# Two experts' lists instead of two ranks' lists, with tokens handed on from the lower expert's chunk to the higher one's list

## The chip, the cores and the metric

The kernel runs on one core of one Trainium2 chip. A core has a matrix engine (PE, with its weight loads listed as PEld), a vector engine (DVE), a scalar engine (ACT), GpSimd (POOL) and a sync engine (SP) that here only issues transfers. PE writes to PSUM banks, DMA moves data between DRAM and SBUF. The metric is the device time of one launch in microseconds, lower is better. Each launch computes the whole layer for one seed.

## The reference

```python
xn = _layernorm(x)                                         # x: 3125 x 256
x = x + gnn(xn, src, dst) + linear_attention(xn)           # 53125 edges, 8 heads
tokens = _layernorm(x)
probs = softmax(tokens @ router_w.T)                       # 8 experts
rw, re = top_k(probs, 2); rw = rw / rw.sum(-1)
out = tokens
for e in range(8):
    h = gelu(tokens @ w1[e] + b1[e])                       # 256 x 256, exact gelu
    out = out + combine[:, e:e + 1] * (h @ w2[e] + b2[e])
x = x + out
```

So a token's result is a sum of three parts: x + tokens, and two experts' outputs, each with its weight. The order of the two experts does not matter.

## The kernel before, in words

**Up to 283 us** the first layernorm, the projections, the edge counts and the graph sum are worked out. `rows` [125, 25, 261] keeps all tokens: token `t * 125 + p` is in row p of tile t.

**Routing (283 to 328 us)** goes over six groups of up to five tiles (`ROUT`). For a group DVE adds the graph part (`add_graph`), takes mean and variance (`scale`), picks the two best experts (`choose`: max, max_index, and `oh`, a one-hot of each rank's expert), and works out where in a list each token stands (`weigh`: `slot_i`, one row number for rank 0 and one for rank 1). A row of `rows` holds 256 normalized values, the token's number, its two weights and what undoes the normalization (std + 1, mean). POOL sends tile t with `send(t, r2)` (L545): an indirect transfer that writes each of 125 rows at its own row number in the DRAM table `xs`, one region for each rank. A list of an expert starts and ends on whole chunks of 128 rows, filled up with rows `null` that SP stored during the graph stage (L390); a null row carries a token number that is out of bounds, so that it is written nowhere. After each group's rank 0 sends one rank 1 send follows (`BETWEEN`), after the last group eight (up to `EARLY` = 13), and the other 12 stand in POOL's queue behind the chunks 0, 2, ... 22.

**The table (322 to 328 us)**: on one partition DVE turns the counts of each expert's tokens into an expert and a first row for each of 64 chunks (L1089 to L1121), then `table_done`.

**The expert stage (from 339.7 us)** runs 64 chunks, `MC` = 32 for rank 0 and then 32 for rank 1. 3125 tokens in eight lists never need more than 32 chunks; what the data do not need are null chunks, which take the same steps. For chunk c: SP reads its first row into a register (L393) and loads 128 rows into one of six buffers `xch` (L396), which it may do once `ys_done` says that chunk c - 6 was weighed. The first load waits for all rank 0 sends to have landed (`sent[0]`). PE transposes the rows (`turn_rows`, L1471), runs the first layer (L1482) after the turn of the next chunk but one, and the second (L1491, L1493). ACT copies the transposed rows (L693), applies gelu (L701) and, in the first half, undoes the normalization in the buffer (`restore`, L707). DVE copies the weights of the chunk after next (L1131, L1132) and weighs (`weigh_rows`): L1142 takes the token numbers, L1144 writes restored row + weight x output into `ys` (L1147 weight x output alone in the second half). POOL writes `ys` to `out` (`add_rows`): L560 plainly in the first half, L563 as an adding transfer in the second, once all of the first half's have landed. PE's program fixes the order: at step c it turns chunk c + 2, runs the first layer of c + 1 and the second of c. `keep_clock` (L1167) are matmuls without use, 20 of them behind `table_done`, ahead of the first turn.

## Time and profile before

| what | us |
|---|---|
| median of three runs (492.91 to 498.22) | 496.13 |
| the profiled execution | 495.52 |
| its span in the profile | 493.8 |
| PE busy | 443.1 |
| DVE busy | 320.3 |
| ACT busy | 282.8 |
| POOL busy | 238.0 |

The span runs from the first to the last instruction of the program; the profiled execution's own time is 1.7 us longer. Busy shares are averages over stages with different limits, so the stages have to be looked at one by one. PE is the busiest engine, but its matmuls are pipelined and their ends are modelled, so what PE waits for, and what waits for PE, says more than its busy time.

### The profile page before, as it was taken

How to read it: one execution, taken by the hardware profiler on the slowest of the kernel's cores; microseconds unless marked ns; L12 is line 12 of the kernel's file. 1: busy time of each engine (PE TensorE's matmuls, PEld its weight loads, DVE VectorE, ACT ScalarE, POOL GpSimd, SP SyncE). 2: the span in 40 equal slices, each digit the busy share in tenths (PEclk: the TensorE clock that was granted, in tenths of full speed). 3: DMA queues.
4: the chain of work that ended last, by engine and by line, in shares of the span. 5: the costliest groups of instructions: out<-in, count | busy, mean ns of one | idle time of the engine just before them, and what ended most of it. 6: DMA issues, size and time to landing. Idle time of an engine off the chain costs nothing.

```text
span 493.8 us, 10033 instructions
## 1 busy us (share of the span) xinstructions
PE 443.1 (90%) x3289; PEld 327.2 (66%) x3289; DVE 320.3 (65%) x869; ACT 282.8 (57%) x632; POOL 238.0 (48%) x261
## 2 busy tenths in 40 slices
PE   2899999989999999999989997845998989999993
PEld 1787787755666665556645655614877878999982
DVE  3687779687777777677713897570655656666662
ACT  2757455757777776777734686403655547444441
POOL 5057683481111111111100057887676764688886
PEclk9999999999999999999998989658999999999998
DMA  8844005554777776576670013335444443367763
GB/s 217 178 134 133 13 16 171 174 134 120 150 150 150 150 151 156 144 145 134 134 133 2 1 49 91 87 87 147 122 129 132 125 130 98 81 110 123 118 104 36
DMA packets 119300, 57.52 MB, mean 116 GB/s; under 512 B 92647, under 2 KB 116435, under 8 KB 119248
## 3 DMA queue, kind: packets, MB, share of 16 engines
q1 hardware_dynamic: 104688, 41.63, 35.9%
q0 software_dynamic: 13744, 14.39, 14.4%
q10 hardware_dynamic: 816, 0.85, 0.7%
q8 instruction: 27, 0.44, 0.4%
q14 instruction: 25, 0.20, 0.1%
HBM read 19.14 MB, written 19.14 MB: 78 GB/s over the span
## 4 chain that ended last, share of the span: by engine, by line
PE 73%; DVE 7%; DMA 6%; issue 4%; ACT 4%; POOL 3%; SPq 1%; POOLq 0%; another core or an unknown queue 0%; DVEq 0%; ACTq 0%
PE bank L1482 12%; PE bank L1273 12%; PE bank L1493 11%; PE bank L1224 9%; PE bank L1304 4%; PE bank L1191 4%; PE bank L1200 3%; PE bank L1471 3%; DMA region_a<-region_a 3%; PE bank L1207 2%; PE bank L1167 2%; DMA rows<-in_x 2%; PE bank L1491 2%; PE bank L1284 2%; POOL xs L545 2%
## 5 line engine op out<-in xcount | busy, mean ns | idle before, releaser
L615 ACT CAST region_a<-bank 128x500 bf16<-128x500 f32 (+1 forms) x175 | 112.2, 668 | 46.1 <-PE bank L1224 41.9
L545 POOL DMA_INDIRECT xs<-rows,slot_i x50 | 61.9, 1237 | 49.8 <-issue 44.3
L1273 PE MATMUL bank<-region_a,region_z 125*64 125x500 bf16 (+1 forms) x525 | 71.1, 367 | 2.6 <-DMA region_a<-region_a 2.6
L1482 PE MATMUL bank<-region_a,region_c 128*128 128x128 f32 x512 | 70.1, 280 | 2.9 <-issue 2.0
L516 POOL COPY wide<-den 125x256 f32<-125x256 f32 x25 | 12.9, 516 | 119.4 <-DVE den L923 119.4
L1224 PEld LDWEIGHTS bank<-region_a 128*128 128x128 bf16 x625 | 41.2, 101 | 42.6 <-issue 31.0
L1482 PEld LDWEIGHTS bank<-region_a,region_c 128*128 128x128 f32 x512 | 63.3, 194 | 5.7 <-issue 3.8
L1224 PE MATMUL bank<-region_a 128*128 128x125 bf16 x625 | 64.8, 220 | 1.6 <-ACT region_a L615 1.3
L1493 PE MATMUL bank<-region_c,region_a 128*128 128x256 f32 x256 | 65.7, 379 | 0.0
L701 ACT ACTIVATE region_a<-bank,region_c 128x128 f32<-128x128 f32 x128 | 40.3, 367 | 40.7 <-PE bank L1482 28.4
L563 POOL DMA_INDIRECT out<-region_a x32 | 55.4, 1730 | 12.4 <-issue 8.5
L1131 DVE COPY region_c<-region_w 128x1026 f32 x64 | 46.9, 733 | 17.1 <-issue 16.3
L693 ACT COPY region_a<-bank 128x256 f32<-128x256 f32 x64 | 24.0, 375 | 44.8 <-issue 23.0
L1493 PEld LDWEIGHTS bank<-region_c,region_a 128*128 128x128 f32 x256 | 43.7, 190 | 4.0
L862 DVE TENSOR_TENSOR region_a<-iota,locs 128x3200 bf16<-128x3200 bf16 x25 | 45.9, 1835 | 0.0
L560 POOL DMA_INDIRECT out<-region_a x32 | 33.1, 1035 | 24.8 <-DVE region_a L1144 14.6
L856 DVE TENSOR_TENSOR region_a<-iota,keys 128x3150 bf16<-128x3150 bf16 x25 | 44.7, 1790 | 0.0
L1142 DVE CAST region_a<-region_a 128x1 int32<-128x1 f32 x64 | 9.8, 153 | 50.3 <-issue 33.4
L1273 PEld LDWEIGHTS bank<-region_a,region_z 125*64 125x64 bf16 x525 | 24.8, 110 | 22.3 <-DMA region_a<-region_a 3.2
L1167 PE MATMUL bank<-zeros,ones 128*128 128x512 bf16 x108 | 31.9, 447 | 6.8 <-DVE expert_i L1121 6.8
L1191 PE MATMUL bank<-wzkv,region_a 128*125 128x320 f32 x100 | 32.2, 445 | 0.0
L465 POOL TENSOR_SCALAR rows<-rows,rstd,shift 125x256 f32<-125x256 f32 x25 | 19.2, 776 | 23.6 <-DVE region_a L749 23.5
(219 smaller groups left out, 764.9 us busy)
## 6 DMA issues: line engine op xcount, KB each, us to landing
region_a<-xs SPq DMA_DIRECT2D x64, 130.5 KB
region_w<-in_w SPq DMA_DIRECT2D x4, 1024.0 KB, 9.1
rows<-in_x SPq DMA_DIRECT2D x5, 560.0 KB
xs<-null SPq DMA_DIRECT2D x16, 130.5 KB
xs<-null SPq DMA_DIRECT2D x2, 913.5 KB
out<-region_a POOLq DMA_INDIRECT x64
xs<-rows,slot_i POOLq DMA_INDIRECT x50
wzkv<-in_WkvT ACTq DMA_DIRECT2D x1, 512.0 KB, 6.4
```

What stands on the lines that cost most here:

```text
L545: nc.gpsimd.indirect_dma_start(xs, bass.IndirectOffsetOnAxis(slot_i[:, t, r2:r2 + 1], 0), rows[:, t, :], None).then_inc(sent[r2], 16)
L563: nc.gpsimd.indirect_dma_start(out, to, ys[:, c % 4, :], None, bounds_check=N - 1, oob_is_err=False, compute_op=ALU.add).then_inc(added[c ...
L615: nc.scalar.copy(to, count_bank(n)[:, 0:w * TP].rearrange("p (c t u) -> p c t u", c=w, t=NT)).then_inc(adj_done, 1)
L856: nc.vector.tensor_tensor(koh[:, t % 2, :, :].rearrange("p c (m u) -> p c m u", u=2), counting(KW), columns(keys, t, KW), ALU.is_equal).th ...
L862: nc.vector.tensor_tensor(loh[:, t % 2, :, :].rearrange("p c (m u) -> p c m u", u=2), counting(P), columns(locs, t, P), ALU.is_equal).then ...
L1131: nc.vector.tensor_copy(wc[:, c % 3, :].rearrange("p (a f) -> p a f", a=1), w_all[:, bass.ds(e, 1), :])
L1167: nc.tensor.matmul(ps[:], ones16[:], zeros[:], start=True, stop=True)
L1191: last = nc.tensor.matmul((y0, y1)[s][0:TP, 0:H1 + D], xnT[:, s, k, :], wzkv[:, k, 0:H1 + D], start=(k == 0), stop=(k == 1))
L1224: last = nc.tensor.matmul(count_bank(n)[:, (c - lo) * TP:(c - lo + 1) * TP], loh[:, t % 2, c, :], koh[:, t % 2, c, 0:TP], start=True, stop ...
L1273: last = nc.tensor.matmul(block_out(b), zparts[:, t, part, :], adjT[0:TP, t % 2, lo:hi, 0:TP], start=False, stop=False, skip_group_check=True)
L1482: last = nc.tensor.matmul(hid_ps[c % 2][:, f * P:(f + 1) * P], wc[:, c % 3, k * D + f * P:k * D + (f + 1) * P], xT[:, c % 2, k * P:(k + 1) ...
L1493: last = nc.tensor.matmul(y_ps[c % 2][:, 0:D], hT[:, c % 2, f * P:(f + 1) * P], wc[:, c % 3, (2 + f) * D:(3 + f) * D], start=False, stop=( ...
```

## The change

The lists are no longer by rank, but by number: a token stands in the list of its lower numbered expert in the first half and in that of the higher in the second. Expert 7 is never the lower one and expert 0 never the higher, so seven lists remain in a half, and 31 chunks suffice. `rows` carries, besides the token's number, the row in the second half's lists (`NEXT`) and the two weights by number. Only the first half's rows are sent from `rows`, 25 sends in all. After its first expert a chunk's rows, with a partial result of 256 values behind them, are written straight from the chunk's buffer into the second lists (`xs_next`, 518 values in a row, by `hand_on`); the second half loads them from there, adds the second expert's part in the same buffer and writes the sum to `out` plainly. `ys` is gone. There are eight buffers, and a load waits until the buffer's last write has landed (`added`). A load of the second half also waits until as many first-half chunks have landed as DVE worked out for it (`need_of`, against `landed`, which POOL raises three chunks behind).

```diff
+MC = 31
...
-BETWEEN, EARLY = 1, 13
+BEHIND = 3
 EARLY_COUNTS = {21: (0,), 22: (1, 2), 23: (3, 4), 24: (5, 6)}
-XB = 6
+XB = 8
...
+    xs = nc.dram_tensor("xs", (RR, ROW), F32, kind="Internal").ap()
+    xs_next = nc.dram_tensor("xs_next", (RR, WIDE), F32, kind="Internal").ap()
...
-        ys = r.take(P, 4 * D).rearrange("p (s d) -> p s d", s=4)
-        xch = r.take(P, XB * ROW).rearrange("p (s d) -> p s d", s=XB)
...
                     r2, e = divmod(t - 2, NX)
-                    at = r2 * RR + e * CAP
-                    sp.dma_start(xs[at:at + P, :], null[:]).then_inc(nulls_stored, 16)
+                    to, w = ((xs, ROW), (xs_next, WIDE))[r2]
+                    sp.dma_start(to[e * CAP:e * CAP + P, :], null[:, 0:w]).then_inc(nulls_stored, 16)
 
             def load_chunk(c):
-                at = sp.value_load(row_of[0:1, c:c + 1], min_val=0, max_val=2 * RR - P)
+                at = sp.value_load(row_of[0:1, c:c + 1], min_val=0, max_val=RR - P)
                 if c >= XB:
-                    sp.wait_ge(ys_done, c - XB + 1)
-                sp.dma_start(xch[:, c % XB, :], xs[bass.ds(at, P), :]).then_inc(xch_in[c % XB], 16)
+                    sp.wait_ge(added[c % XB], c // XB * 16)
+                if c < MC:
+                    sp.dma_start(xch[:, c % XB, 0:ROW], xs[bass.ds(at, P), :]).then_inc(xch_in[c % XB], 16)
+                else:
+                    sp.wait_ge(landed, sp.value_load(need_of[0:1, c - MC:c - MC + 1], min_val=1, max_val=MC))
+                    sp.dma_start(xch[:, c % XB, :], xs_next[bass.ds(at, P), :]).then_inc(xch_in[c % XB], 16)
...
-            sp.wait_ge(sent[0], NT * 16)
+            sp.wait_ge(sent, NT * 16)
             for c in range(NCH):
-                if c == MC:
-                    sp.wait_ge(sent[1], NT * 16)
                 load_chunk(c)
...
-            def send(t, r2):
-                nc.gpsimd.indirect_dma_start(xs, bass.IndirectOffsetOnAxis(slot_i[:, t, r2:r2 + 1], 0),
-                                             rows[:, t, :], None).then_inc(sent[r2], 16)
+            def send(t):
+                nc.gpsimd.indirect_dma_start(xs, bass.IndirectOffsetOnAxis(slot_i[:, t, 0:1], 0),
...
                 for t in range(lo, hi):
-                    send(t, 0)
-                for t in range(g * BETWEEN, (g + 1) * BETWEEN if g < NR - 1 else EARLY):
-                    send(t, 1)
-
-            def add_rows(c):
+                    send(t)
+
+            def hand_on(c):
                 pool.wait_ge(ys_done, c + 1)
-                to = bass.IndirectOffsetOnAxis(to_row[:, c:c + 1], 0)
-                if c < MC:
-                    nc.gpsimd.indirect_dma_start(out, to, ys[:, c % 4, :], None, bounds_check=N - 1, oob_is_err=False
-                                                 ).then_inc(added[c % 4], 16)
-                else:
-                    nc.gpsimd.indirect_dma_start(out, to, ys[:, c % 4, :], None, bounds_check=N - 1, oob_is_err=False,
-                                                 compute_op=ALU.add).then_inc(added[c % 4], 16)
-
-            for c in range(NCH):
-                if c == MC:
-                    for s in range(4):
-                        pool.wait_ge(added[s], MC // 4 * 16)
-                add_rows(c)
-                if c % 2 == 0 and c // 2 + EARLY < NT:
-                    send(c // 2 + EARLY, 1)
+                nc.gpsimd.indirect_dma_start(xs_next, bass.IndirectOffsetOnAxis(to_row[:, c:c + 1], 0),
+                                             xch[:, c % XB, :], None, bounds_check=RR - 1, oob_is_err=False
+                                             ).then_inc(added[c % XB], 16)
+
+            def write_rows(c):
+                pool.wait_ge(ys_done, c + 1)
+                nc.gpsimd.indirect_dma_start(out, bass.IndirectOffsetOnAxis(to_row[:, c:c + 1], 0),
+                                             xch[:, c % XB, PART:WIDE], None, bounds_check=N - 1, oob_is_err=False
+                                             ).then_inc(added[c % XB], 16)
+
+            def pass_on(c):
+                pool.wait_ge(added[c % XB], (c // XB + 1) * 16)
+                pool.sem_inc(landed, 1)
...
+            for c in range(MC):
+                hand_on(c)
+                if c >= BEHIND:
+                    pass_on(c - BEHIND)
+            for c in range(MC - BEHIND, MC):
+                pass_on(c)
+            for c in range(MC, NCH):
+                write_rows(c)
...
-                nc.scalar.activation(xch[:, s, 0:D], xch[:, s, 0:D], ACT.Identity, scale=xch[:, s, D + 3:D + 4],
-                                     bias=xch[:, s, D + 4:D + 5]).then_inc(restored, 1)
+                nc.scalar.activation(xch[:, s, PART:WIDE], xch[:, s, 0:D], ACT.Identity,
+                                     scale=xch[:, s, SPAN:SPAN + 1], bias=xch[:, s, MEAN:MEAN + 1]).then_inc(restored, 1)
...
+                for r2, (order, pick) in enumerate(((ALU.is_lt, ALU.min), (ALU.is_gt, ALU.max))):
+                    nc.vector.tensor_tensor(first[:, 0:n, r2], top_atf[:, 0:n, 0], top_atf[:, 0:n, 1], order)
+                    last = nc.vector.tensor_tensor(role[:, 0:n, r2], top_atf[:, 0:n, 0], top_atf[:, 0:n, 1], pick)
+                chain(last)
...
                 for r2 in range(2):
                     last = nc.vector.tensor_tensor(oh[:, 0:n, r2, :], iota_x[:, 0:n, :],
-                                                   top_atf[:, 0:n, r2:r2 + 1].to_broadcast([TP, n, NX]), ALU.is_equal)
+                                                   role[:, 0:n, r2:r2 + 1].to_broadcast([TP, n, NX]), ALU.is_equal)
...
+                nc.vector.tensor_tensor(first[:, 0:n, :], first[:, 0:n, :], of_both(ex, n), ALU.max)
                 chain(nc.vector.tensor_scalar(exs[:, 0:n], ex[:, 0:n], 1.0, None, ALU.add))
-                chain(nc.vector.reciprocal(rows[0:TP, lo:hi, D + 1], exs[:, 0:n]))
-                chain(nc.vector.tensor_tensor(rows[0:TP, lo:hi, D + 2], rows[0:TP, lo:hi, D + 1], ex[:, 0:n], ALU.mult))
+                chain(nc.vector.reciprocal(exs[:, 0:n], exs[:, 0:n]))
+                nc.vector.tensor_tensor(rows[0:TP, lo:hi, W_LOW:W_HIGH + 1], first[:, 0:n, :], of_both(exs, n), ALU.mult)
...
-                nc.vector.tensor_copy(slot_i[0:TP, lo:hi, :], slot_f[:, 0:n, :]).then_inc(slot_done, 1)
+                nc.vector.tensor_copy(rows[0:TP, lo:hi, NEXT], slot_f[:, 0:n, 1])
+                nc.vector.tensor_copy(slot_i[0:TP, lo:hi, :], slot_f[:, 0:n, 0:1]).then_inc(slot_done, 1)
...
+            nc.vector.tensor_tensor(passed_by, past[:, 1, :, :], ends[:, 0:1, :].to_broadcast([1, MC, NX]), ALU.mult)
             chain(nc.vector.tensor_reduce(expert_f[:], past[:], AX_X, ALU.add))
+            chain(nc.vector.tensor_reduce(need[:], passed_by, AX_X, ALU.max))
+            nc.vector.tensor_scalar(need_of[:], need[:], 1.0, None, ALU.max)
...
             def weigh_rows(c):
                 s = c % XB
                 dve.wait_ge(y_ready, c + 1)
+                goal, weight = (NEXT, W_LOW) if c < MC else (TOKEN, W_HIGH)
+                nc.vector.tensor_copy(to_row[:, c:c + 1], xch[:, s, goal:goal + 1])
                 if c < MC:
                     dve.wait_ge(restored, c + 1)
-                if c >= 4:
-                    dve.wait_ge(added[c % 4], c // 4 * 16)
-                nc.vector.tensor_copy(to_row[:, c:c + 1], xch[:, s, D:D + 1])
-                if c < MC:
-                    nc.vector.scalar_tensor_tensor(ys[:, c % 4, :], y_ps[c % 2][:, 0:D], xch[:, s, D + 1:D + 2],
-                                                   xch[:, s, 0:D], ALU.mult, ALU.add).then_inc(ys_done, 1)
-                else:
-                    nc.vector.tensor_scalar(ys[:, c % 4, :], y_ps[c % 2][:, 0:D], xch[:, s, D + 2:D + 3], None,
-                                            ALU.mult).then_inc(ys_done, 1)
+                nc.vector.scalar_tensor_tensor(xch[:, s, PART:WIDE], y_ps[c % 2][:, 0:D], xch[:, s, weight:weight + 1],
+                                               xch[:, s, PART:WIDE], ALU.mult, ALU.add).then_inc(ys_done, 1)
```

On POOL, at the end of the routing and into the first half. Before, with `send` as L545 and the write to `out` as L560:

```order
L545 DMA xs<-rows,slot_i 53888x261 [waits slot_done,tk_done]
L545 DMA xs<-rows,slot_i 53888x261 x10
L560 DMA out<-region_a 3125x256 [waits ys_done]
L545 DMA xs<-rows,slot_i 53888x261
L560 DMA out<-region_a 3125x256 [waits ys_done] x2
```

Now, with `send` as L554 and `hand_on` as L565:

```order
L554 DMA xs<-rows,slot_i 26816x262 [waits slot_done,tk_done]
L554 DMA xs<-rows,slot_i 26816x262 x2
L565 DMA xs_next<-region_a 26816x518 [waits ys_done] x4
L565 DMA xs_next<-region_a 26816x518 [waits added0,ys_done]
L565 DMA xs_next<-region_a 26816x518 [waits added1,ys_done]
```

Three sends stand in the last group instead of eleven, none among the chunks, and from the fifth chunk on POOL waits for an earlier write to land before it goes on.

On SP, the last load before the halves meet and the first after it. Before:

```order
L393 TENSOR_LOAD row_of
L393 ISA x2
L396 ISA [waits ys_done]
L396 DMA region_a<-xs 128x261
L393 TENSOR_LOAD row_of [waits sent1]
```

Now:

```order
L403 ISA [waits added6]
L403 DMA region_a<-xs 128x262
L399 TENSOR_LOAD row_of
L399 ISA x2
L405 TENSOR_LOAD need_of [waits added7]
L405 ISA x2
L406 ISA [waits landed]
L406 DMA region_a<-xs_next 128x518
```

A load waits for a landed write instead of a weighed chunk, and one of the second half reads a second register and waits twice.

On DVE, in `choose`. Before:

```order
L1045 CAST top_atf<-top_at 125x10 [waits diff_done]
L1049 TENSOR_TENSOR oh<-iota_x,top_atf 125x5x8 [waits pos_ready,dve_step]
L1049 TENSOR_TENSOR oh<-iota_x,top_atf 125x5x8
```

Now:

```order
L1059 CAST top_atf<-top_at 125x10 [waits diff_done]
L1061 TENSOR_TENSOR first<-top_atf 125x5 [waits dve_step]
L1062 TENSOR_TENSOR role<-top_atf 125x5
L1061 TENSOR_TENSOR first<-top_atf 125x5
L1062 TENSOR_TENSOR role<-top_atf 125x5
L1067 TENSOR_TENSOR oh<-iota_x,role 125x5x8 [waits pos_ready,dve_step]
```

Four small instructions and one more chained wait stand ahead of `oh`.

## Rows read from the trace of the kernel before

**Rows 1.** The page's first part: span.
```profile
span 493.8 us, 10033 instructions
```

**Rows 2.** Windows: stretch; its us; PE, PEld, DVE, ACT, POOL busy; PEclk, DMA share, GB/s.
```profile
300.00:328.00 28.00, 17.05 (x108) 12.19 (x109) 19.26 (x116) 11.59 (x22) 22.38 (x19) 0.74 0.33 88
...
347.20:409.00 61.80, 56.13 (x377) 48.62 (x376) 36.42 (x101) 35.23 (x101) 42.06 (x37) 1.00 0.44 126
409.00:422.00 13.00, 13.00 (x93) 11.81 (x92) 8.69 (x26) 8.80 (x25) 6.71 (x7) 1.00 0.34 96
422.00:486.00 64.00, 63.82 (x454) 57.96 (x452) 41.62 (x120) 29.73 (x89) 52.17 (x31) 1.00 0.66 106
```

**Rows 3.** Chain of waits, 318 to 345: start us, us, what.
```profile
331.49 4.34 DMA xs<-rows,slot_i
...
338.08 2.69 DMA region_a<-xs
```

**Rows 4.** Timeline around the start of the expert stage: start, us, instruction, idle before.
```profile
317.72 0.17 DVE L1069 CAST slot_i<-slot_f 125x10 int32<-125x10 f32 x1
...
328.00 7.28 PE L1167 MATMUL bank<-zeros,ones 128*128 128x512 bf16 x20 [6.81 <-DVE expert_i L1121]
...
339.74 0.44 PE L1471 MATMUL bank<-ident,region_a 128*128 128x128 f32 x2 [4.46 <-DMA region_a<-xs]
...
341.29 1.91 PE L1482 MATMUL bank<-region_a,region_c 128*128 128x128 f32 x8
...
343.60 1.19 POOL L545 DMA_INDIRECT xs<-rows,slot_i  x1 [0.30 <-issue]
```

**Rows 5.** Timeline: DVE's small instructions of the routing and of the table.
```profile
293.82 0.31 DVE L1049 TENSOR_TENSOR oh<-iota_x,top_atf 125x40 bf16<-125x40 f32 x2
...
323.39 0.75 DVE L1103 TENSOR_TENSOR region_a<-ends,chunk_of 1x256 f32<-1x256 f32 x2
...
324.18 0.67 DVE L1107 TENSOR_REDUCE expert_f<-region_a 1x64 f32<-1x512 f32 x1
```

**Rows 6.** Line L1142 in 340:421, then 421:494: ns min/median/max, first and last start.
```profile
L1142 DVE CAST region_a<-region_a x32: 145/154/156, 345.8 to 420.0; 128x1 int32<-128x1 f32 x32
...
L1142 DVE CAST region_a<-region_a x32: 153/154/155, 422.2 to 486.0; 128x1 int32<-128x1 f32 x32
```

**Rows 7.** Timeline: chunk 5 of the first half, and a matmul group from its undisturbed end.
```profile
353.37 1.44 POOL L545 DMA_INDIRECT xs<-rows,slot_i  x1 [0.30 <-issue]
...
354.98 0.63 ACT L701 ACTIVATE region_a<-bank,region_c 128x128 f32<-128x128 f32 x2 [2.37 <-remote]
...
411.59 1.06 PE L1482 MATMUL bank<-region_a,region_c 128*128 128x128 f32 x8
```

**Rows 8.** Waits in 346:409: engine and line, for whom: us in total, times, longest.
```profile
DVE region_a L1142 <- issue: 19.0, 19, 2.0
...
ACT region_a L701 <- remote: 8.6, 4, 2.5
```

**Rows 9.** Lines of the indirect transfers on POOL: ns min/median/max, first and last start.
```profile
L485 POOL DMA_INDIRECT region_c<-in_dst,row_i x5: 1214/1214/1647, 38.6 to 45.1; - x5
...
DMA to landing us min/median/max: 4.5/4.5/4.5
...
L545 POOL DMA_INDIRECT xs<-rows,slot_i x50: 1187/1192/1719, 283.7 to 403.1; - x50
...
L560 POOL DMA_INDIRECT out<-region_a x32: 976/1007/1245, 347.2 to 421.3; - x32
...
L563 POOL DMA_INDIRECT out<-region_a x32: 1549/1777/2020, 425.3 to 488.6; - x32
```

**Rows 10.** Line L393, SP's register load: ns min/median/max.
```profile
L393 SPq TENSOR_LOAD <-row_of x64: 263/272/753, 335.9 to 473.4; - x64
```

**Rows 11.** Timeline: the last chunk.
```profile
486.02 0.15 DVE L1142 CAST region_a<-region_a 128x1 int32<-128x1 f32 x1 [0.43 <-PE bank L1493]
...
488.57 1.55 POOL L563 DMA_INDIRECT out<-region_a  x1 [0.30 <-issue]
```

More of the change, by code:

```diff
@@ L27 @@
 CB = 2 * TP
-ROW = D + 5
+ROW = D + 6
+PART, WIDE = ROW, ROW + D
+TOKEN, NEXT, W_LOW, W_HIGH, SPAN, MEAN = range(D, D + 6)
 W = 5
@@ L48 @@
 RR = NX * CAP + NULLS * P
-NOWHERE = 4096.0
+NOWHERE = 65536.0
 CTX0 = 128
@@ L244, in build @@
         top_atf = sb("top_atf", [TP, J, 2])
+        role = sb("role", [TP, J, 2])
+        first = sb("first", [TP, J, 2])
         ex = sb("ex", [TP, J])
```

41 lines of the change are left out of this document (23 added, 18 removed).

## Prediction

> **What bounds the kernel now.** I read the page first, then windows by stage, then inside the stages the chain of waits and the timeline. The span is 493.8 us [rows 1]; the profiled execution took 495.52, so 1.7 us lie around it. The change leaves the graph stage alone but for wider null stores, so the place to look is behind 283 us.
>
> *Start of the expert stage.* POOL sends are the chain there. The last rank 0 send starts at 331.49 and lands 4.34 us later, and only then does SP issue loads [rows 3]; PE reads the first rows at 339.74, after 4.46 us of waiting for that load [rows 4]. So 8.25 us (339.74 - 331.49) lie between the start of the last send and PE's start. A send costs POOL 1.19 us and a gap of 0.30, 1.49 together [rows 4, 9]. POOL is behind: the fifth group's rows are known at 317.89 (317.72 + 0.17), and the last rank 0 send comes 13.6 us later. A second road to the same point: `table_done` at 328.00 releases 20 `keep_clock` matmuls, 7.28 us, to 335.28 [rows 4].
>
> *The halves.* In the window 409 to 422 and from 422 to 486 PE is busy all the time (13.00 of 13.00, 63.82 of 64.00) [rows 2]: PE is the bound, and the second half's 32 chunks are weighed from 422.2 to 486.0, 2.06 us apart; its last two are shorter, and I take 2.09 for one in the steady flow. The first half's 32 are weighed from 345.8 to 420.0, 74.2 us for 31 steps or 2.39 each [rows 6]. So the first half loses about 74.2 - 31 x 2.09 = 9.4 us, and all of it before 409. There ACT's gelu and DVE's weighing wait late for PE (8.6 us in four waits, 19.0 in nineteen) [rows 8]; at 354.98 gelu starts after 2.37 us of waiting, while a send stands on POOL just before it, taking 1.44 instead of 1.19 [rows 7, 9]. What differs after 409 is that no rank 1 send is left (the last starts at 403.1 [rows 9]); loads and writes to `out` go on. So the sends are the likely cause, though not through the amount: with the adding writes the DMA share is 0.66 and nothing stalls, with the sends it is 0.44 [rows 2].
>
> **The change, part by part.** *(1) Five sends less ahead of the last one.* POOL catches up before the fifth group, so the path becomes: the group's rows known, then eight sends. DVE's `choose` gets four small instructions (three at some 0.08, one with its chained wait 0.2, by the pair of L1049 that takes 0.31 [rows 5]), about 0.45; `weigh` about 0.15. On DVE's own stretches of this stage that shows once or one and a half times, elsewhere waits for ACT cover it: the fifth group's rows come 0.9 us later, 318.8. First send 0.2 later, the eighth 7 x 1.49 after it: 329.4 instead of 331.49, gain 2.1; with the same 8.25 us behind it PE starts at 337.65. Bounds: 3.0 if DVE's additions stay covered, 0 if they show in all groups. The table gets three instructions, 0.4 (one of L1103's two), some 0.35 (half of L1107) and 0.2, so 0.95, and is late by 0.9 + 0.6 from before: 330.4, and `keep_clock` ends at 337.7. Both roads end together, so a later table would eat the gain.
>
> *(2) PE does not idle ahead of the first chunk.* The first layer's eight matmuls take 1.91 us at 341.29 against 1.06 later [rows 4, 7], behind the 4.46 us of idling. With PE kept at work up to the first turn I count 1.0 us for this and the group after it; between 0 and 1.2.
>
> *(3) Two chunks less:* 2 x 2.09 = 4.2 us, since PE is the bound in both halves.
>
> *(4) No sends among the chunks.* If the stalls go with them, 9.4 us. What takes their place is one write of 128 rows x 2072 bytes for each chunk (27 of 31 hold rows; I counted the lists from the reference's inputs: 5, 6, 5, 3, 4, 2, 2 chunks low, 1, 2, 2, 4, 5, 6, 8 high). POOL's price: a transfer of 1024 bytes a row takes 1.01, one of 1044 bytes 1.19, one of 1700 bytes 1.21 [rows 9], so the size hardly counts; 1.0 to 1.8 (L563), plus 0.3, under 2.09 or just at it. DMA: share 0.34 at 409 to 422, where half of the chunks are null; a full chunk of load and plain write is nearer 0.45, and twice the bytes in one of them makes about 0.6, under the 0.66 that ran without a stall.
>
> *(5) A buffer is free when its write has landed.* From weighing on: 0.63 for DVE, 0.3, then landing 4.5 at most (L485's 4.5, the send's 4.34), SP's second register load and its checks about 0.7 with 0.35 for the issue [rows 10], the load 2.69, in the second half some 0.5 more for twice the bytes: 9.7. Eight buffers give 8 x 2.09 = 16.7, less the time from a chunk's turn to its weighing, three steps and a little (6.5): 10.2. It fits by 0.5. Before, six buffers gave 6.0 for 3.8. The `landed` wait never holds: the first load of the second half needs 5 landed chunks and is issued behind chunk 23, the load of chunk 40 needs 23. Queued behind `pass_on` on POOL is the next `hand_on`, whose write three chunks ago (6.3 us) has landed. SP's own turn, two register loads of 0.27 [rows 10] with their checks, the wait and the issue, is 1.9 us by my estimate, under 2.09.
>
> A rule speaks against this part. The Trainium skill ("DMA: Bandwidth & Descriptors", Anatomy of one DMA) says that most of a transfer's fixed 2 us is the receipt of the write, that DRAM is the slowest target, and that the bytes add 1 us for 436 KB. By it a hand-on would land 2.6 us after its issue, less than the 4.5 that I took from the row; its warning of a surprisingly long receipt is the case of the late buffer below, which would need 5.0 us.
>
> *(6) The end.* The last weighing starts at 486.02 and POOL ends at 490.12 [rows 11], behind an adding write of 1.55. Plain writes of 1.0 leave no backlog: 0.63 + 0.14 + 1.0 = 1.8 instead of 4.1, gain 2.3. The wider null stores hide behind the transposes; nothing counted.
>
> **Sum:** 2.1 + 1.0 + 4.2 + 9.4 + 2.3 = 19.0. Span 474.8, with 1.7 around it 476.5; the median of before is 0.6 above its profiled execution, so 477.
>
> **Rivals.** *(A) Half of the stalls stay.* The hand-ons are scattered writes of odd-sized rows into a table in DRAM, as the sends are, and writes to `out` are not. If each costs half of what a send costs now (9.4 / 12 = 0.78), 27 x 0.39 = 10.5 come back: 487.5. *(B) Each hand-on stalls like a send:* 27 x 0.78 = 21: 498, no change. *(C) The stall goes with the bytes,* 1.55 for each hand-on, twice a send's: 42 us, and 519, slower. The point from which the sign turns is (19.0) / 27 = 0.70 us for each hand-on. Against (B) and (C): writes of 128 rows to `out` and even adding ones run without a stall, and the 16 null stores of 1044 byte rows did no harm. For (A): I know the cause only by its company. *(D) A late buffer or a full POOL.* If landing takes 6 us, the turn is (11.2 + 6.5) / 8 = 2.21, and 0.12 x 62 = 7.5 us are lost; a hand-on of 2.1 + 0.3 on POOL loses 0.3 x 27 = 8: 485. *(E)* The null stores or the table eat more than I allow, 480 to 484, a variant of (D).
>
> One thing raises the forecast over (A). While sends run alone, from 300 to 328, the DMA share is 0.33 [rows 2], as if only 5.3 of the 16 engines worked at a time. The Trainium skill ("DMA: Bandwidth & Descriptors", Why a DMA increments its semaphore by 16) says that the number of engines is the largest up to 16 that divides the rows: 5 for 125 rows, 16 for 128. The trace agrees with 5. By that rule a send fills a few engines with 25 rows each and a hand-on does not, which favours the case without stalls; it changes no term.
>
> **Chances.** Forecast (472 to 482) 0.55; (A) 0.20; (D) and (E) 0.13; (B) 0.07; (C) 0.05. The range must leave out no more than 0.2: 472 to 489 holds the first three less their edges. A measurement of this kernel can tell about 1%, 5 us: faster 0.87, within 1% 0.08, slower 0.05.
>
> **What would show it.** PE's first turn near 337.7 with little waiting; weighings 2.09 apart in both halves, gelu's late waits gone; 62 weighings; POOL's hand-ons near 1.0; SP's loads of the second half released by a landed write, never by `landed`; the last POOL write 2 us behind the last weighing. Wrong if the first half's steps stay above 2.2, if PE waits for loads, or if the table ends after 331.

## Result and the profile after

The changed kernel takes 478.65 us in the median (476.46 to 482.35), beside 496.98 (492.91 to 498.22) for the kernel before in the same group of runs: a ratio of 0.965, 95% interval 0.960 to 0.970. The profiled execution took 476.46, with 1.7 us around its span. In a later group of runs it was 478.94 in four executions, beside 496.91: 0.967 (0.961 to 0.973). Medians here are of all runs of a kernel; ratios and their intervals leave out the runs that lie more than 1.5% above its fastest. The forecast was 477.

The span first, then the windows by stage (stretch; its us; busy time of PE, PEld, DVE, ACT, POOL; PEclk, DMA share, GB/s), which answer to [rows 1] and [rows 2]:

```profile
span 474.7 us, 10025 instructions
...
346.00:409.00 63.00, 63.00 (x455) 57.92 (x454) 41.67 (x121) 42.92 (x117) 29.71 (x30) 1.00 0.59 179
422.00:466.00 44.00, 43.96 (x313) 39.90 (x312) 28.09 (x83) 20.50 (x62) 21.08 (x22) 1.00 0.62 166
```

PE is now busy all the time in the first half too (63.00 of 63.00, where it had been 56.13 of 61.8), although the DMA share went up from 0.44 to 0.59 and the transfer rate from 126 to 179 GB/s. The line of the weighing in the first and in the second half (ns min/median/max, first and last start) answers to [rows 6]:

```profile
L1165 DVE CAST region_a<-region_a x31: 153/153/155, 339.4 to 402.0; 128x1 int32<-128x1 f32 x31
...
L1165 DVE CAST region_a<-region_a x31: 153/154/155, 404.3 to 466.7; 128x1 int32<-128x1 f32 x31
```

Thirty steps are 2.09 us each in the first half (62.6) and 2.08 in the second (62.4). The waits in 346 to 409 (engine and line, for whom, us in total, times, longest) answer to [rows 8]:

```profile
ACT region_a L715 <- PE bank L1503: 15.2, 29, 0.6
DVE region_a L1165 <- PE bank L1514: 11.8, 26, 0.5
...
DVE region_a L1165 <- issue: 1.5, 3, 0.6
```

The gelu's four waits of about 2 us without a releaser on the core are gone, and the weighing's 19.0 us of such waits are 1.5. Now the start of the expert stage, by the timeline; it answers to [rows 4], with the lines of `slot_i` (L1092) for the fifth and the sixth group:

```profile
314.24 0.16 DVE L1092 CAST slot_i<-slot_f 125x5 int32<-125x5 f32 x1
...
316.14 1.19 POOL L554 DMA_INDIRECT xs<-rows,slot_i  x1 [0.30 <-issue]
...
318.81 0.16 DVE L1092 CAST slot_i<-slot_f 125x3 int32<-125x3 f32 x1
...
325.37 6.84 PE L1188 MATMUL bank<-zeros,ones 128*128 128x512 bf16 x20 [7.22 <-DVE expert_i L1147]
...
326.64 1.57 POOL L554 DMA_INDIRECT xs<-rows,slot_i  x1 [0.30 <-issue]
...
334.11 0.44 PE L1492 MATMUL bank<-ident,region_a 128*128 128x128 f32 x2 [1.90 <-DMA region_a<-xs]
```

PE's first turn is at 334.11 instead of 339.74. And the end, with POOL's last three transfers, answering to [rows 11], and the line on which the program's closing drains are counted:

```profile
463.98 0.48 DVE L1168 SCALAR_TENSOR_TENSOR region_a<-bank,region_a 128x256 f32<-128x256 f32 x1
...
465.25 0.97 POOL L571 DMA_INDIRECT out<-region_a  x1 [1.09 <-DVE region_a L1168]
...
466.82 0.47 DVE L1168 SCALAR_TENSOR_TENSOR region_a<-bank,region_a 128x256 f32<-128x256 f32 x1
467.11 0.97 POOL L571 DMA_INDIRECT out<-region_a  x1 [0.89 <-DVE region_a L1168]
468.39 0.98 POOL L571 DMA_INDIRECT out<-region_a  x1 [0.30 <-issue]
```
```profile
L61 POOLq DRAIN  x1: 6647/6647/6647, 467.9 to 467.9; - x1
```

POOL is done at 469.37 (468.39 + 0.98), but the span ends at 474.7. A drain of POOL's queue, 6.65 us long, lasts to within 0.2 us of it.

So the two spans differ by 19.1 us, which the traces divide like this:

| | before | after | gain | forecast |
|---|---|---|---|---|
| PE's first turn | 339.74 | 334.11 | 5.6 | 2.1 |
| from there to the first weighing | 6.1 | 5.3 | 0.7 | 1.0 |
| first to last weighing (64 and 62 chunks) | 140.2 | 127.3 | 12.9 | 13.6 |
| last weighing to the end | 7.8 | 8.0 | -0.2 | 2.3 |
| sum | | | 19.1 | 19.0 |

The sum is right to 0.1 us because errors cancel: the start brought 3.5 us more than forecast, the end 2.5 less, and the two rows between them 1.0 less.

### The profile page after: what moved, and what is told of

Its sections match the earlier page's. It is cut to its first block, busy times and chain, and to the rows that moved or that the text cites. A ratio compares the mean times of both kernels' runs of the same rounds, so it can differ in the third digit from the quotient of the medians.

```text
span 474.7 us, 10025 instructions
## 1 busy us (share of the span) xinstructions
PE 432.2 (91%) x3259; PEld 320.2 (67%) x3259; DVE 317.6 (67%) x900; ACT 281.7 (59%) x625; POOL 180.6 (38%) x235
## 4 chain that ended last, share of the span: by engine, by line
PE 77%; DMA 6%; ACT 5%; DVE 4%; issue 3%; POOL 3%; SPq 1%; POOLq 0%; ACTq 0%; DVEq 0%
PE bank L1294 12%; PE bank L1503 11%; PE bank L1514 11%; PE bank L1245 9%; PE bank L1325 4%; PE bank L1212 4%; PE bank L1221 4%; PE bank L1188 4%; PE bank L1492 3%; DMA region_a<-region_a 3%; PE bank L1228 2%; DMA rows<-in_x 2%; PE bank L1440 2%; PE bank L1305 2%; PE bank L1512 1%
## 5 line engine op out<-in xcount | busy, mean ns | idle before, releaser
L1294 PE MATMUL bank<-region_a,region_z 125*64 125x500 bf16 (+1 forms) x525 | 69.8, 361 | 2.4 <-DMA region_a<-region_a 2.4
L1245 PE MATMUL bank<-region_a 128*128 128x125 bf16 x625 | 64.8, 220 | 1.7 <-ACT region_a L629 1.4
L1503 PE MATMUL bank<-region_a,region_c 128*128 128x128 f32 x496 | 65.8, 275 | 0.0
L1514 PE MATMUL bank<-region_c,region_a 128*128 128x256 f32 x248 | 63.7, 379 | 0.0
L1503 PEld LDWEIGHTS bank<-region_a,region_c 128*128 128x128 f32 x496 | 60.2, 191 | 0.4
L525 POOL COPY wide<-den 125x256 f32<-125x256 f32 x25 | 12.9, 516 | 119.4 <-DVE den L937 119.4
L1157 DVE COPY region_c<-region_w 128x1026 f32 x62 | 43.2, 697 | 16.8 <-issue 16.7
L565 POOL DMA_INDIRECT xs_next<-region_a x31 | 31.1, 1003 | 45.1 <-DVE region_a L1168 37.4
L554 POOL DMA_INDIRECT xs<-rows,slot_i x25 | 30.3, 1211 | 45.1 <-issue 36.2
L1514 PEld LDWEIGHTS bank<-region_c,region_a 128*128 128x128 f32 x248 | 42.3, 190 | 4.0
L571 POOL DMA_INDIRECT out<-region_a x31 | 31.2, 1007 | 33.8 <-DVE region_a L1168 26.1
L967 DVE TENSOR_TENSOR qn<-bank,region_q 128x250 f32<-128x250 f32 x25 | 10.5, 419 | 29.6 <-PE bank L1305 27.4
```

The costliest lines, as they stand in the source:

```text
L571: nc.gpsimd.indirect_dma_start(out, bass.IndirectOffsetOnAxis(to_row[:, c:c + 1], 0), xch[:, c % XB, PART:WIDE], None, bounds_check=N - 1, ...
L1157: nc.vector.tensor_copy(wc[:, c % 3, :].rearrange("p (a f) -> p a f", a=1), w_all[:, bass.ds(e, 1), :])
L1245: last = nc.tensor.matmul(count_bank(n)[:, (c - lo) * TP:(c - lo + 1) * TP], loh[:, t % 2, c, :], koh[:, t % 2, c, 0:TP], start=True, stop ...
L1294: last = nc.tensor.matmul(block_out(b), zparts[:, t, part, :], adjT[0:TP, t % 2, lo:hi, 0:TP], start=False, stop=False, skip_group_check=True)
L1503: last = nc.tensor.matmul(hid_ps[c % 2][:, f * P:(f + 1) * P], wc[:, c % 3, k * D + f * P:k * D + (f + 1) * P], xT[:, c % 2, k * P:(k + 1) ...
L1514: last = nc.tensor.matmul(y_ps[c % 2][:, 0:D], hT[:, c % 2, f * P:(f + 1) * P], wc[:, c % 3, (2 + f) * D:(3 + f) * D], start=False, stop=( ...
```

## Experiments

All times are medians; each group of runs was made on one chip beside its own runs of the kernel before. An unexpected number comes first, since everything below has to be read with it: **the kernel before itself takes 496 to 497 us in some groups and 489 in others.** It was 496.98 beside the kernel after, 488.95 in the first group of experiments, 496.91 in the second, 496.16 in the third, 489.06 in the fourth. The second and the fourth group ran on the same chip, so it isn't the chip alone. The kernel before has no profile in a group of 489; what is said of late results there rests on the other kernels. I call them groups of 497 and of 489.

| group of | kernel | us | kernel before | first half: weighings that start in 335 to 409 | us a step |
|---|---|---|---|---|---|
| 489 | a_send125 | 483.08 | 488.95 | 31 in 65.8 | 2.19 |
| 489 | a_null128 | 482.44 | 488.95 | 32 in 66.7 | 2.15 |
| 489 | b_between0 | 496.82 | 488.95 | 29 in 60.1 | 2.15 |
| 489 | a_xb6 | 512.74 | 488.95 | 27 in 68.2 | 2.62 |
| 497 | before_again | 497.70 | 496.91 | 26 in 60.6 | 2.42 |
| 497 | after_again | 478.94 | 496.91 | 33 in 66.9 | 2.09 |
| 497 | a_send125_2 | 489.84 | 496.91 | 29 in 66.7 | 2.38 |
| 497 | b_plain | 496.71 | 496.91 | 25 in 56.7 | 2.36 |
| 497 | b_pad128 | 505.78 | 496.16 | 24 in 56.3 | 2.45 |
| 497 | a_pad128 | 483.22 | 496.16 | 32 in 64.8 | 2.09 |
| 489 | a_null128_2 | 482.47 | 489.06 | 31 in 63.4 | 2.11 |
| 489 | a_null1024 | 482.08 | 489.06 | 32 in 65.5 | 2.11 |

### Do the sends make the stalls?

**a_send125**: the kernel after, with twelve sends of the old kind between the chunks of the first half.

```diff
             for c in range(MC):
                 hand_on(c)
+                if c % 2 == 0 and c < 24:
+                    nc.gpsimd.indirect_dma_start(aside, bass.IndirectOffsetOnAxis(slot_i[:, 13 + c // 2, 0:1], 0),
+                                                 rows[:, 13 + c // 2, :], None).then_inc(set_aside, 16)
```

> The kernel after, and behind every second hand_on of the first half (chunks 0 to 22) one send more on POOL, of 125 rows x 1048 bytes from rows to a table in DRAM that nobody reads: twelve sends at the places where the kernel before had them. The result is that of the kernel after. Theory S (a send while chunks run makes PE's results come late, whatever else runs): the first half's steps grow by about 0.78 us for each send, 9 us in all, gelu's waits of about 2 us with no releaser on the core come back, and the time is about 487. Rival P (it was the late rank 1 sends' region, or the kernel before's four output buffers, and sends as such do no harm): steps stay at 2.09, 478. Rival Q (POOL becomes the bound, 4.1 us of transfers for two chunks of 4.18, and buffers come late): PE waits for loads, not gelu for PE; 480 to 490.

Measured: 483.08. In its profile no gelu waits 2 us for PE; the steps are 2.19. What lengthens them is what the expectation calls rival Q, in a small measure: PE waits for chunks to be loaded. The waits in 341 to 409:

```profile
PEld bank L1497 <- DMA region_a<-xs: 2.7, 5, 1.1
PEld bank L1497 <- DMA region_a<-xs_next: 0.7, 1, 0.7
```

That looked as if the sends made no late results, but the kernel before was at 489 in this group. So the same kernel was run again with both kernels beside it.

> The kernel before, unchanged, profiled on the chip on which the other kernels of this group run. In the first group of experiments it took 489.0 us where it had taken 497.0 beside the kernel after, and none of their four profiles has one of the late PE results of about 2 us. Theory C (the late results belong to the chip or the session, not to the sends): where this kernel takes 489, its profile has no gelu wait of 2 us and first half steps of 2.1 to 2.2; where it takes 497, it has them. Theory S (the sends bring them): it has about ten of them in either case, and the 8 us lie elsewhere.

> The kernel after, unchanged, on the same chip. By theory C, where the kernel before takes 489 the gain is the 19 us less the 9.4 of the stalls and less what the late result at 305.20 cost: 478, a gain of 8 to 11. Where the kernel before takes 497: 478, a gain of 18. By theory S the gain is 18 or 19 on both.

> The kernel after with twelve sends of 125 rows between the chunks of the first half, as in a_send125, now beside the kernel after itself. By theory S it is 9 us slower than the kernel after. By theory C it is slower by what sends cost without late results: in a_send125 the first half's steps were 2.09 but for some 0.1 to 0.9 us at a third of the chunks, 3 us in all, and the drain at the end was 1 us longer: 3 to 4 us slower on a chip without late results; on a chip with them both kernels could have them.

This group was one of 497. The waits in 346 to 409 of the kernel before, run again, then of the kernel after, run again, then of the one with twelve sends:

```profile
DVE region_a L1142 <- issue: 18.8, 20, 2.0
...
ACT region_a L701 <- remote: 8.2, 5, 2.2
```
```profile
DVE region_a L1165 <- issue: 1.1, 2, 0.6
```
```profile
DVE region_a L1170 <- remote: 6.8, 3, 2.8
ACT region_a L720 <- remote: 3.7, 2, 2.6
```

and one such place in the timeline of the last:

```profile
348.62 1.21 POOL L584 DMA_INDIRECT aside<-rows,slot_i  x1 [0.30 <-issue]
348.76 0.63 ACT L720 ACTIVATE region_a<-bank,region_c 128x128 f32<-128x128 f32 x2 [1.15 <-remote]
...
349.59 0.15 DVE L1170 CAST region_a<-region_a 128x1 int32<-128x1 f32 x1 [1.99 <-remote]
```

With the sends back, the kernel after is 10.9 us slower than without in the medians of all runs (489.84 against 478.94) and 10.1 in those of the runs that the ratios count (489.04); the intervals, 0.979 to 0.989 and 0.961 to 0.973 of the kernel before, don't meet. The late results and the steps of 2.4 are back with them. In the profiled executions it is 9.9 (spans of 486.5 and 476.6): 8.9 in the halves, since the last weighing starts 135.9 us behind the first (477.5 - 341.6) instead of 127.0 (468.6 - 341.6), and 1.0 behind the last weighing. That is 8.9 / 12 = 0.74 us for each send; 8.2 of the 8.9 are in the first half, where the sends are, and this is the number to set beside the prediction's 9.4: 0.68 for each send, and 0.78 from the kernel before. So in the groups of 497 the sends do cost about what was claimed. In the group of 489 the same twelve sends cost little: from the steps (30 x 0.10) and the longer end (1.0), an estimate of 4 us, and the steps' part is the loads above, not late results. The condition that makes the difference is not in the kernel, and no run shows what it is.

The traces show one more difference between the two kinds of group. In all eight profiles of a group of 497 (also those of the kernels before and after), at least 120 to 163 of the 1803 or 1820 semaphore updates that the engines' instructions make have no record in the packed trace; in all six of a group of 489 none of these is missing. So a wait that is put down to "remote" or "issue" in a group of 497 may owe that name to a missing record, and whether the recording itself has a part in the 8 us is not known. The steps don't depend on it: they are differences of starts.

**Which property of a send?** The prediction, in its argument over (A), had leaned on the 125 rows of a send. **b_pad128** and **a_pad128** make them 128 (a_pad128's edit; b_pad128's is the same for both ranks):

```diff
-        rows = sb("rows", [TP, NT, ROW])
+        rows_all = sb("rows", [P, NT, ROW])
+        rows = rows_all[0:TP]
...
-        slot_i = sb("slot_i", [TP, NT, 1], I32)
+        slot_i = sb("slot_i", [P, NT, 1], I32)
...
+            sp.dma_start(rows_all[TP:P, :, 0:D], a["x"][0:(P - TP) * NT].rearrange("(p t) d -> p t d", t=NT)).then_inc(pads_in, 16)
...
+            nc.gpsimd.memset(slot_i[:], int(NOWHERE))
...
-                                             rows[:, t, :], None).then_inc(sent, 16)
+                                             rows_all[:, t, :], None, bounds_check=RR - 1, oob_is_err=False
+                                             ).then_inc(sent, 16)
...
+            pool.wait_ge(pads_in, 16)
```

> The kernel before with every send made of 128 rows instead of 125: three more partitions in rows, whose place in slot_i is out of bounds, so that the same 125 rows are written. The result is unchanged. Theory E (the sends make PE's results late because 125 rows go over five DMA engines, 128 over sixteen): the late results go, in the first half 9 us, ahead of it 2 to 3 us, and the landing of the last send gets 1 to 2 us shorter: where the kernel before takes 497, this takes 484 to 487; where it takes 489 (no late results there) it takes 486 to 488. Rival R (any transfer of POOL with rows of 1048 bytes does it): 497, steps as before. Rival N (the rows that are left out, or the bound, cost POOL more): POOL's send takes over 1.19 us, and the start is later by 18 times the difference.

> The kernel after with the same edit, 128 rows in each of the 25 sends. The result is unchanged. Theory E: the late results in the routing stage go (a_send125_2 and the repeated kernel after had two to four of up to 1.24 us there), and a send lands in 2.5 to 3.5 us instead of 4.25: PE's first turn 1 to 3 us earlier, at 332 to 333.5, total 476 to 478 for 478.9. Rival R: the landing is unchanged, 479. Rival N: as above, later.

Measured: 505.78 beside 496.16, ratio 1.022 (1.014 to 1.029), and 483.22 for the kernel after with the edit, 0.976 (0.969 to 0.982). b_pad128 is slower than the kernel before. For a_pad128 that is not shown: the kernel after did not run in its group, and the interval meets that of after_again (0.961 to 0.973). In both profiles about 3 us more than without the edit lie behind POOL's last transfer (7.2 and 8.2 us to the end of the span, for 3.7 and 5.4), so the steps tell more here than the totals. A send does get cheaper on POOL, but the late results stay in b_pad128's first half, and longer ones turn up in the routing stage of both. POOL's line of b_pad128 and its waits in 346 to 409; then, in a_pad128, the copy of the transposes (the line that is L669 before and L683 after):

```profile
L549 POOL DMA_INDIRECT xs<-rows,slot_i x50: 971/973/1438, 284.0 to 407.9; - x50
```
```profile
DVE region_a L1148 <- issue: 20.0, 14, 3.0
```
```profile
309.60 1.05 ACT L688 COPY region_a<-bank 128x500 f32<-128x500 f32 x2 [2.54 <-remote]
```

Theory E is out: with 128 rows the steps are 2.45, as bad as with 125. So is the argument that the share of 0.33 tells five engines from sixteen: while padded sends run back to back, in 314 to 321 of b_pad128, the share is 0.26, not far from it.

```profile
314.00:321.00 7.00, 6.32 (x49) 4.63 (x48) 3.07 (x27) 4.46 (x9) 5.48 (x6) 1.00 0.26 93
```

The Trainium skill ("DMA: Bandwidth & Descriptors", Why a DMA increments its semaphore by 16 and not by 1) gives sixteen engines to 128 rows and five to 125. No run shows the number of engines. POOL's 0.97 for 1.19 us is a difference between the two kinds of send, but neither the stalls nor the time followed from it: the measurement decides against its use here.

The rest of the question went to transfers that share a send's place and length but not its source, and that have 128 rows and a bound on the row number, **a_null128** and **a_null128_2** (the same kernel), and **a_null1024** (1024 bytes a row into a table with rows of 1024 bytes):

```diff
+                if c % 2 == 0 and c < 24:
+                    nc.gpsimd.indirect_dma_start(aside, bass.IndirectOffsetOnAxis(to_row[:, c:c + 1], 0), null[:, 0:ROW],
+                                                 None, bounds_check=RR - 1, oob_is_err=False).then_inc(set_aside, 16)
```

> The kernel after with twelve transfers more at the same places, of the same row length, 1048 bytes, but of 128 rows instead of 125, from the constant tile null to the rows that the chunk's hand_on names, in a table that nobody reads. The result is that of the kernel after. If 125 rows are what hurts (few DMA engines with 25 rows each, the share of 0.33 with sends alone): no stalls, 478. If any second scattered transfer beside the chunk's own hurts: as much as the run with 125 rows, about 487. POOL's time for each is 1.0 to 1.2.

> The kernel after with twelve transfers more between the chunks of the first half, of 128 rows x 1048 bytes from the constant tile null to the places of the chunk's hand_on, in a table that nobody reads; as a_null128, on another chip. In the group before, sends of 128 rows left the late PE results where they were, so the number of rows is not their cause. What still sets the send apart from the hand_on: that it is issued 0.3 us behind another transfer of POOL, the length of its rows, and its source rows and table. Theory T (two transfers of POOL at once): where the kernel before takes 496 or more, this has late results of up to 2 us and takes 8 to 12 us more than the kernel after, 487 to 491. Rival V (the send's source or table): none, 480 to 482. On a chip where the kernel before takes 489 it tells nothing.

> The same with rows of 1024 bytes into a table whose rows are 1024 bytes apart. If the length of the rows, no multiple of 512 bytes, brings the late results, they go here and stay in a_null128_2: 480 to 482 against 487 to 491. By theory T both are alike. By rival V neither has any.

Measured: 482.44, 482.47 and 482.08, without late results in their profiles. But all three fell into groups of 489, in which real sends make none either (483.08), so they don't tell whether it is two transfers of POOL at once, or what else sets a send apart. They are inconclusive; that stays open.

### The start: sends ahead of the last one

```diff
-BETWEEN, EARLY = 1, 13
+BETWEEN, EARLY = 0, 10
```

> The kernel before with no rank 1 sends among the groups' rank 0 sends (BETWEEN 0 for 1, EARLY 10 for 13): ten follow the last rank 0 send, and fifteen go between the chunks of the first half. The result is unchanged. By the prediction's first step the last rank 0 send starts 2.1 us earlier or more (329.4 for 331.49), since POOL catches up before the fifth group. If the late result at 305.20 (1.77 us) is also a cost of POOL's unbroken run of sends, the fifth group's rows come 2 to 4 us earlier than at 317.72 and the last send starts near 326; PE's first turn then near 334 to 335. If that late result has nothing to do with them, 317.7 stays and the gain is 2.1. In the first half three more sends between chunks: 2 to 3 us more of stalls. Total: 490 to 496.

Measured: 496.82 beside 488.95. Relative to the first group's `slot_i` (285.71 here, 282.49 before) the last rank 0 send starts after 47.1 us instead of 49.0: the 1.9 us are the size of the prediction's 2.1. With the same sends it is 50.0 in before_again and 50.2 in b_plain, so the gain may be up to 3. The fifth group's rows are known 34.7 us after the first group's, beside 35.4 before: 0.7 earlier and not 2 to 4, and it is 34.4 in before_again. The gain doesn't show in the total, because the edit makes its own hole: the last rank 1 send now goes at 412.56, SP must wait for its landing before it loads a chunk of the second half, and PE waits once 9.1 us for that load. It is a reminder of what the register wait on `landed` avoids in the kernel after. The waits of b_between0 in 405 to 425:

```profile
PE bank L1471 <- DMA region_a<-xs: 9.1, 1, 9.1
```

Without that wait it would be at 488, an estimate, about the kernel before. It has fifteen sends among its chunks and no late result.

### The buffers' turn

```diff
-XB = 8
+XB = 6
```

> The kernel after with six chunk buffers instead of eight. By the prediction's fifth step a buffer's turn from the start of a chunk to its next load is 6.5 + 9.7 = 16.2 us, so six buffers give 2.70 us for each chunk instead of 2.09: PE waits for loads, 62 x 0.61 less the first six, about 34 us, 512. If the landing of a write takes 2.5 us and not 4.5, the turn is about 14: 2.35 for each chunk, 15 us, 493. If it is 12.5 or less nothing changes: 478.

Measured: 512.74, on the number. Sixty-one steps in 162.6 us are 2.665 each, so a buffer's turn is 6 x 2.665 = 16.0 us on average, beside 16.2 of the prediction, and eight buffers (16.7) hold it by 0.7 us. The line of the weighing and the waits of a_xb6 in 345 to 500, then the times from a hand-on's start to its landing and from a load's, in the first half:

```profile
L1165 DVE CAST region_a<-region_a x62: 153/154/156, 339.4 to 502.0; 128x1 int32<-128x1 f32 x62
```
```profile
PEld bank L1492 <- DMA region_a<-xs_next: 22.1, 16, 2.8
...
PEld bank L1492 <- DMA region_a<-xs: 14.1, 11, 3.2
```
```profile
L565 POOL DMA_INDIRECT xs_next<-region_a x31: 973/992/1394, 340.8 to 421.8; - x31
...
DMA to landing us min/median/max: 2.1/3.2/5.3
```
```profile
L403 SPq DMA_DIRECT2D region_a<-xs x31: 337/338/694, 332.0 to 407.0; - x31
...
DMA to landing us min/median/max: 2.0/2.3/3.8
```

So the total fits better than its parts. A hand-on lands 3.2 us after its start in the median, and not 4.5, and a load takes 2.3 and not 2.69. On the other side, POOL starts a transfer 0.8 us behind the end of the weighing, and not 0.3 (464.46 to 465.25 in the kernel after), and PE's waits for other chunks' loads lengthen the way from a chunk's turn to its weighing, from 6.5 us in the kernel after to 7.8 here on average. The 2.6 us that the prediction set against its 4.5 lie nearer to the median; with 2.1 to 5.3 neither is a fixed time. So the expectation's reading, that 512 stands for a landing of 4.5 and 493 for one of 2.5, does not hold.

### The end: plain writes alone

```diff
-                    nc.gpsimd.indirect_dma_start(out, to, ys[:, c % 4, :], None, bounds_check=N - 1, oob_is_err=False,
-                                                 compute_op=ALU.add).then_inc(added[c % 4], 16)
+                    nc.gpsimd.indirect_dma_start(out, to, ys[:, c % 4, :], None, bounds_check=N - 1, oob_is_err=False
+                                                 ).then_inc(added[c % 4], 16)
```

> The kernel before with plain writes to out in the second half instead of adding ones: the low expert's part of each token is left out of the result. By the prediction's sixth step POOL's backlog of one transfer at the end goes, and the end is 2.3 us earlier. In the profile of the kernel after POOL did end 2.0 us instead of 3.6 behind the last weighing, yet the program ended 7.4 us behind it instead of 7.2, with a drain of POOL that begins 0.5 us behind the last weighing and lasts 6.4 to 6.6. If that drain sets the end, this kernel takes as long as the kernel before, within 1 us, its span ends 7.2 to 7.4 behind the last weighing, and no stage is shorter.

Measured: 496.71 beside 497.70 for before_again, with ratios 0.999 (0.995 to 1.003) and 1.002 (0.999 to 1.006). The span ends 5.7 us behind the end of the last weighing, against 7.2 in before_again, so neither expectation held in full: plain writes shorten the end by 1.5 us, not by 2.3 and not by nothing, and 1.5 us drown in the measurement. b_plain's second half overwrites what the first wrote, so that part of each token's sum is missing in its result; its steps are those of the kernel before. The drains of before_again and of b_plain:

```profile
L58 POOLq DRAIN  x1: 6436/6436/6436, 487.5 to 487.5; - x1
```
```profile
L58 POOLq DRAIN  x1: 4931/4931/4931, 489.9 to 489.9; - x1
```

What the kernel after gives back is another piece. From POOL's last transfer to the end of the span it is 3.7 us in before, before_again and b_plain, but 5.4 in after, after_again and a_xb6, 6.4 with twelve transfers more, 3.2 in b_between0, and 7.2 and 8.2 in b_pad128 and a_pad128. That number is the same to 0.1 us in all kernels of one of these sets, in groups of 497 and of 489 alike, so it goes with the kernel. It is not the number of transfers alone: b_between0 has as many as the kernel before, in another order, and 0.5 us less. I found no rule in it.

## Why the prediction was right, and where it was not

**(1) Start, forecast 2.1, measured 5.6: under-sized, and one sentence of it wrong.** "POOL catches up before the fifth group" didn't happen: POOL's last wait for rows is ahead of the fourth group. The fifth group's rows were forecast for 318.8, and were known at 314.40 (314.24 + 0.16), 3.5 us earlier than in the kernel before, while DVE's four new instructions did cost their few tenths. POOL was then still sending group four (first send of group five at 316.14), so the chain is 13 sends, from 308.66 to 326.64 with 1.5 each, and not eight behind a late group. That puts the last send at 326.64 for the forecast 329.4, 2.8 us of the error; the other 0.8 is that PE's first turn follows its start by 7.5 us (334.11 - 326.64) instead of the 8.25 that were taken over. What made the fifth group earlier can be read in ACT's copy of the transposes, before and then after:

```profile
307.05 1.05 ACT L669 COPY region_a<-bank 128x500 f32<-128x500 f32 x2 [1.85 <-remote]
```
```profile
305.20 1.05 ACT L683 COPY region_a<-bank 128x500 f32<-128x500 f32 x2
```

It looks like a late PE result of the same kind as in the first half; that the sends make it is not shown, since the only test, b_between0, ran in a group of 489. The prediction named this wait nowhere; it stands in the trace of before in the middle of the unbroken run of sends, and the reasoning that it applied behind 347 should have been applied at 305 too. The repeated pair agrees: first turn at 340.82 and 335.24, 5.6 again, of which 5.0 are the last send's start (332.88 and 327.88), with the fifth group's rows 1.8 us earlier. There the same copy waits only 0.84 us, in before_again, so the gain does not hang on that wait. The table's road ended at 332.2 (325.37 + 6.84) and not at 337.7, 1.9 us ahead of PE's first turn, so it did not limit.

**(2) First chunk, forecast 1.0, measured 0.7.** Right within its bounds, though PE did idle, 1.9 us instead of 4.46.

**(3) Two chunks less, 4.2.** Right: the steps are 2.09 in both kernels when nothing stalls.

**(4) The stalls, forecast 9.4, measured 8.7** (12.9 less 4.2). The place and the price were right: the first half alone gave 9.5 (74.18 us for 31 steps, then 62.63 for 30, less one step of 2.09), and the second half gave 0.7 less than its one step. The hand-ons (0.99 us on POOL, line below, against 1.0 to 1.8 forecast) bring no stall in a first half with 31 of them: rivals (A), (B) and (C) each wanted 0.39 us or more for one. One late result is left in the second half, at 411.30. Its wait is 2.35 us, but the three steps around it take 0.7 more than three of 2.09.

```profile
L565 POOL DMA_INDIRECT xs_next<-region_a x31: 976/992/1229, 340.8 to 403.4; - x31
...
411.30 0.63 ACT L715 ACTIVATE region_a<-bank,region_c 128x128 f32<-128x128 f32 x2 [2.35 <-remote]
```

The prediction knew the cause "only by its company". The twelve sends put back turn the company into a cause in a group of 497; the groups of 489 show that it is only half of it. Which property of a send it is stays open. The five-engine argument that raised the forecast over (A) was wrong, though the forecast was not.

**(5) Buffers, no loss.** Right, and tested: 16.0 us a turn for 16.2, with terms that err both ways, as a_xb6 shows. Rival (D) needed more than 16.7. `landed` never held SP: the line that waits for it is L406, and it is not among the waits of SP's queue in 389 to 470, which are the closing one and L405's, for the buffer's own write:

```profile
SPq L414 <- DMA out<-region_a: 11.4, 1, 11.4
SPq L405 <- DMA out<-region_a: 8.4, 13, 1.6
```

**(6) End, forecast 2.3, measured -0.2: wrong.** Two steps failed. The first is "plain writes of 1.0 leave no backlog", with 1.8 us from the start of the last weighing to POOL's end. It is 2.6 (466.75 to 469.37): a transfer starts 0.8 us behind the end of the weighing and not 0.14, and the last one still waits 0.3 for the one before it, because the last two chunks are weighed only 0.98 us apart. So POOL gave back 1.5 us (4.1 less 2.6), as in b_plain. The second is "POOL ends at 490.12", taken as the end of the program. 3.7 us more had always stood between POOL's last transfer and the end of the span, [rows 1] against [rows 11], and the prediction took that rest as fixed. It is not: it grew by 1.7 us, and 1.5 less 1.7 are the -0.2.

The forecast was thus right in its largest terms, and right in the sum by luck: 3.5 us too little at the start against 3.5 too much in the other terms, 2.5 of them at the end. How much of the 18 us would be left in a group of 489 was not measured: the kernel after did not run in one. An estimate from a_send125 (483.08, less 3 us of steps, less 1 at the end) is 479, and one from a_null1024 (482.08, less 1 at the end; its halves are as long as after_again's) is 481, which makes the gain 8 to 10 there.

## What to carry to other kernels

When a stage's time is blamed on transfers that happen to run beside it, look for the same symptom in every other stage where they run, and put the transfers back into the new kernel, beside the old kernel in the same group of runs: that gives the price of one. Compare only within such a group, since an unchanged kernel moved by 8 us between groups. And when the end of a program is costed, subtract the last transfer from the span first, and treat that rest as a term of its own.

## Unexpected of the hardware

- PE's results come late for ACT and DVE, with waits of up to 3.0 us among the chunks, where PE itself waits for no DMA. It is so nearly always while POOL issues scattered transfers close together (the one at 411.30 in the kernel after and one at 433.8 in b_plain stand among plain writes to `out` alone), and only in some groups of runs: 497 against 489 us for the same kernel, both on one chip. The Trainium skill ("Perfetto Trace Analysis", Tensor Engine Instruction) says that the end of a matmul in a trace is a model and not a measurement. No run here shows whether the matmuls themselves took longer or only their semaphore was late; by that rule the trace can't tell the two apart.
- A scattered transfer of 128 rows costs POOL 0.97 us, one of 125 rows of the same length 1.19; twice the bytes (2072 a row) cost 0.99. So the length did not count. Whether the number of rows did is not shown: in all kernels here the transfers of 128 rows have a bound on the row number (`bounds_check`) and those of 125 have none, and the edit of b_pad128 and a_pad128 changed both at once.
- The time from POOL's last transfer to the end of the program is between 3.2 and 8.2 us, the same in two profiles of one kernel, and longer by 1.0 with twelve transfers more.
